# One attention and mixture-of-experts layer: the last weighing ahead of four scatters, the routing tables interleaved with the experts' inner values, two waits of TensorE moved

## The reference

```python
x = x + attention(layernorm(x))
x = x + experts(layernorm(x))
```

```python
sim1 = q @ k_l.T ; sim2 = q_l @ k_l.T ; sim3 = q_l @ k.T
attn1, attn2, attn3 = softmax(sim1), softmax(sim2), softmax(sim3)
out = attn1 @ pinv(attn2) @ (attn3 @ v)     # pinv: 6 Newton-Schulz steps
out = out + conv(out)                        # 13 taps along the tokens, per head
out = out.reshape(b, n, 1024) @ w_fc + b_fc
```

## Time and profile before

| | us |
|---|---|
| median of three runs | 1142.69 |
| lowest and highest | 1137.94, 1143.32 |
| the profiled execution, its own time | 1141.43 |
| its span, first to last instruction | 1139.7 |
| mean granted TensorE clock over the span | 0.992 |
| TensorE busy | 1093.7 |
| VectorE busy | 634.5 |
| ScalarE busy | 303.3 |
| GpSimd busy | 301.2 |

### The profile page before, as it was taken

How to read it: one execution, slowest core, us unless ns; L and a number is a source line. 1 busy time by engine, 2 the same in 40 slices (tenths; PEclk the granted TensorE clock), 3 DMA queues, 4 the chain that set the end, 5 groups by cost and what they waited for, 6 DMA issues and landing times.

```text
span 1139.7 us, 22844 instructions
## 1 busy us (share of the span) xinstructions
PE 1093.7 (96%) x9168; PEld 908.3 (80%) x9168; DVE 634.5 (56%) x1353; ACT 303.3 (27%) x457; POOL 301.2 (26%) x298
## 2 busy tenths in 40 slices
PE   4999999999989999999999999889999999999996
PEld 4887888888888756766776767768888888899996
DVE  7467666555478575686677677662323333244442
ACT  4433223332234422332243233221111111111110
POOL 6000000000200022234643553542232332334343
PEclk9999999999999999999999999899999999999999
DMA  9200000001200040322322134343333333321321
GB/s 340 112 1 1 1 1 1 1 1 38 58 3 0 22 167 28 104 75 61 137 75 85 66 98 131 108 131 76 50 50 51 47 53 48 42 39 36 47 25 12
DMA packets 48540, 68.94 MB, mean 60 GB/s; under 512 B 7872, under 2 KB 41792, under 8 KB 47424
## 3 DMA queue, kind: packets, MB, share of 16 engines
q1 hardware_dynamic: 34720, 47.50, 13.1%
q0 software_dynamic: 13296, 16.92, 8.7%
q10 hardware_dynamic: 432, 3.24, 0.7%
HBM read 42.10 MB, written 26.46 MB: 60 GB/s over the span
## 4 chain that ended last, share of the span: by engine, by line
PE 88%; DVE 6%; issue 2%; POOL 2%; ACT 1%; POOLq 0%; DVEq 0%
PE ps L1770 21%; PE ps L1793 11%; PE ps L1641 10%; PE ps L1694 10%; PE ps L1353 9%; PE ps L1392 9%; PE ps L1686 5%; PE ps L1507 1%; PE ps L1753 1%; PE ps L1327 1%; PE ps L1526 1%; ACT mem L695 1%; PE ps L1407 1%; PE ps L1608 1%; PE ps L1627 1%
## 5 line engine op out<-in xcount | busy, mean ns | idle before, releaser
L1770 PE MATMUL ps<-mem 128*128 128x256 f32 (+1 forms) x1504 | 260.8, 329 | 0.0
L1770 PEld LDWEIGHTS ps<-mem 128*128 128x128 f32 x1504 | 233.4, 192 | 21.2
L569 POOL DMA_INDIRECT out<-mem x71 | 123.9, 1745 | 256.5 <-DVE mem L1229 190.3
L1793 PE MATMUL ps<-mem 128*128 x568 | 136.9, 385 | 5.7 <-DVE mem L1221 3.4
L1221 DVE TENSOR_TENSOR mem<-mem,ps 128x512 f32<-128x512 f32 x71 | 48.8, 687 | 164.7 <-PE ps L1770 144.7
L539 POOL TENSOR_TENSOR mem<-mem,small 128x1024 f32<-128x1024 f32 x36 | 68.6, 1904 | 238.6 <-DVE small L1158 108.7
L1641 PE MATMUL ps<-mem 128*128 128x512 f32 x288 | 129.7, 594 | 1.3 <-DVE mem L1032 1.3
L775 ACT ACTIVATE mem<-ps 128x512 f32<-128x512 f32 x71 | 42.4, 597 | 316.4 <-PE ps L1770 316.4
L1694 PE MATMUL ps<-mem 128*128 128x256 f32 x512 | 120.7, 390 | 0.0
L1793 PEld LDWEIGHTS ps<-mem 128*128 128x128 f32 x568 | 105.4, 193 | 18.7 <-issue 6.3
L1392 PE MATMUL ps<-mem 128*128 128x256 f32 x512 | 117.5, 383 | 0.6 <-ACT mem L649 0.6
(11 more groups left out here) (226 smaller groups left out, 1291.7 us busy)
## 6 DMA issues: line engine op xcount, KB each, us to landing
mem<-w_gu SPq DMA_DIRECT2D x9, 1024.0 KB, 5.9
mem<-xs_d SPq DMA_DIRECT2D x22, 260.0 KB, 2.8
mem<-x SPq DMA_DIRECT2D x8, 512.0 KB, 8.0
mem<-x SPq DMA_DIRECT2D x32, 128.0 KB, 2.3
out<-mem SPq DMA_DIRECT2D x32, 128.0 KB, 1.7
mem<-w_down SPq DMA_DIRECT2D x8, 512.0 KB, 5.8
xnt_d<-mem ACTq DMA_DIRECT2D x3, 1056.0 KB, 5.0
mem<-xnt_d SPq DMA_DIRECT2D x3, 1056.0 KB, 5.0
```

Of the source, the lines that this page charges most:

```text
L569: pool.indirect_dma_start(out=out_rows, out_offset=bass.IndirectOffsetOnAxis(ap=rows[:, D + 1:D + 2].bitcast(U32), axis=0), in_=ys[:, r % ...
L1770: mm = pe.matmul(bank(2 * c + n % 2)[:, i * size:(i + 1) * size], w[:, k, c, f * P:(f + 1) * P], xst[:, a % 2, k, 0:size], start=(k == 0), ...
L1793: mm = pe.matmul(bank(down_bank(a, b))[:, 0:D], hid[:, u, i * size + b * P:i * size + (b + 1) * P], w_d_s[:, e, f], start=(f == 0), stop=( ...
```

## The change

Five places are edited; no instruction is added or taken away on TensorE, VectorE or GpSimd, apart from where waits stand.

1. GpSimd (line 557 on): the scatters of a step that is 35 or 36 go one step later. By `PLACED` these are the eight DMAs of group 5 and no others. So `weigh(35)` and `add_bias(29)` now stand ahead of the first four of them (tiles 0 and 1 of the group), and `add_bias(30)` ahead of the other four. The two loops over groups and halves change places; the order of all other scatters stays as it was.
2. VectorE: `table` is cut in two, `whole_items` (its first six operations) and `table` (the other ten). For the units, `hidden_out(2)` now stands between the two, where it stood behind both.
3. VectorE: `units_taken` and the tiles' table leave their place ahead of `expert_weights(FIRST + 1)` (item 4) and go behind `hidden_out(5)`, in the first unit. The wait for `d_tiles` goes to the first block of item 23.
4. TensorE, landmark stage: in the turn m = 1, `c1_max_columns(3)` goes from between the halves of `c1_ut(1)` to behind the second.
5. TensorE: the wait for `p_pm` goes from ahead of the first `c2_sim` to ahead of the second.

```diff
@@ gpsimd
+            def sent_at(g, h):
+
+                i = PLACED[g] + (h if g < LATE else 0)
+                return i + 1 if QT - 1 <= i <= QT else i
+
             for i in range(STEPS):
                 if 1 <= i <= QT:
                     weigh(i - 1)
                 if y_tile(i) is not None:
                     add_bias(y_tile(i))
-                for h in range(2):
-                    for g in range(NG):
-                        if PLACED[g] + (h if g < LATE else 0) == i and 2 * h < GROUPS[g][1]:
+                for g in range(NG):
+                    for h in range(2):
+                        if sent_at(g, h) == i and 2 * h < GROUPS[g][1]:
                             scatter(g, 2 * h)
                             scatter(g, 2 * h + 1)
@@ vector
-            def table(rows, up, shift, count, eid, row, done):
+            def whole_items(up, shift):
 
                 ch.link(dve.tensor_scalar(te.bitcast(I32), n_e, float(up), None, ALU.add))
...
                 ch.link(dve.tensor_tensor(te, ends, nt, ALU.subtract))
+
+            def table(rows, eid, row, done):
+
                 ch.link(dve.scalar_tensor_tensor(out=tc, in0=te, scalar=-float(rows), in1=base, op0=ALU.mult, op1=ALU.add))
@@ vector
             sizes()
-            table(2 * P, 0, 8, NU, u_eid, u_row, "d_units")
+            whole_items(0, 8)
             hidden_out(2)
+            table(2 * P, u_eid, u_row, "d_units")
             rows_weighed(0)
...
             hidden_out(3)
-            units_taken()
-            table(P, P - 1, 7, NT, t_eid, t_row, "d_tiles")
             expert_weights(FIRST + 1)
             rows_weighed(1)
             hidden_out(4)
-            dve.wait_ge(s("d_tiles"), 1)
             for n in range(BLOCK[FIRST], NSTEP):
                 a, h = STEP_OF[n]
                 if h == 0:
                     rows_weighed(a - 1)
                 hidden_out(n)
+                if n == BLOCK[FIRST]:
+                    units_taken()
+                    whole_items(P - 1, 7)
+                    table(P, t_eid, t_row, "d_tiles")
+                if a + 2 == FIRST + NU and h == 0:
+                    dve.wait_ge(s("d_tiles"), 1)
@@ tensor, landmark stage
                 c1_ut(m, 0)
-                if more:
+                if more and m > 1:
                     c1_max_columns(m + 2)
...
                 c1_ut(m, 1)
+                if m == 1:
+                    c1_max_columns(m + 2)
@@ tensor, ahead of the token stage
-            pe.wait_ge(s("p_pm"), NQ // 4)
             pe.wait_ge(s("c2_g1a"), NQ // 2)
             pe.wait_ge(s("c2_g1b"), NQ // 2)
...
             def token_step(i):
+                if i == 1:
+                    pe.wait_ge(s("p_pm"), NQ // 4)
                 if i < QT:
                     c2_sim(i)
```

## The result

The changed kernel takes 1134.19 us, the median of six runs (1133.93 to 1135.69); the kernel before has 1142.06 beside it. The ratio is 0.9938, with a 95% interval of 0.9922 to 0.9954: 7.1 us, or 0.62%, less (the two medians are 7.9 us apart). On another occasion, beside the last experiments, it was 0.9935 (0.9919 to 0.9952); one of the eleven runs of the kernel before there took 2291.07 us, and the ratio leaves it out. The forecast was 1135.0.

What follows compares the result with a forecast made beforehand. TensorE, running matmuls for 1093.7 of 1139.7 us, was taken as the bound. Terms -1.2 + 0.4 - 2.05 + 0 - 3.75 = -6.6 gave 1134.8 from 1141.43, stated as 1135.0; range 1131.5 to 1140.0.

Steps and rivals of the forecast that it cites:

- Edit 5, forecast -1.2: Start of token stage: `c2_sim(0)` starts right behind the last projection and the first softmax chain moves along; -1.2 us.
- Edit 4, forecast +0.4: Landmark stage, pair 3's transposes: TensorE wins 1.2 us, then idles some 1.5 waiting for `b_sub`; +0.4 us.
- Edit 1, forecast -2.05: Last convolution and group 7's transposes: scores 3.8 us earlier, less one clock fall of 1.75; -2.05 us.
- bound of no wait for a landing: Group 7's normalising: best case without waiting for scattered data to land and without a clock fall; -5.6 us.
- Edit 2, forecast 0: Ahead of `down(2)`: it still waits for the weighing, and the later `d_units` is covered; 0 us.
- Edit 3, forecast -3.75: Ahead of `down(4)`: it starts 2.0 us earlier and a clock fall of 1.75 goes; -3.75 us.
- a fall of the clock: Behind TensorE's idle spans: where the clock falls, a span costs 1.7 to 3.5 us beyond its length.
- the second rival: Around 721 us: the clock falls for as long as before, since light matmuls follow; 1136.5 us, chance 0.15.
- six idle spans of over 0.9 us: TensorE after start-up: 1.90, 1.35, 2.17, 2.3, 2.43 and 1.0 us, the last touched by no edit.

Runs made afterwards that it cites:

- Edit 1's execution: Only GpSimd's scatters of group 5 put one step later, on the kernel before: ratio 0.9979 (0.9962 to 0.9996).
- The two variants: Changed kernel with pair 3's transposes unmoved and `rows_weighed(0)` ahead of the units' `table`: 0.9895 to the kernel before; the same with `hidden_out(2)` back behind the table: 0.9940.
- The run of edit 5: Only the wait for `p_pm` moved to ahead of the second `c2_sim`, on the kernel before: ratio 0.9978 (0.9966 to 0.999).
- the split: Changed kernel with pair 3's transposes unmoved and the two DMAs of group 5's first tile kept ahead of the last weighing: 1131.24 us, 0.9908 to the kernel before.

## Why the prediction was right

Its sum was -6.6 and the profiled executions give -7.1. That they are so close is in part luck: the changed kernel's other profiled execution spans 1131.0 us, -8.7, because the clock did not fall behind `down(2)`'s wait there. What speaks for the prediction is that each step's mechanism was found. Step by step:

- **Edit 5, forecast -1.2, measured -1.33** in the change and alone. `c2_sim(0)` is right behind the projection, and the softmax chain moved along.
- **Edit 4, forecast +0.4, measured +0.3.** The step that decided it was to follow the chain to `b_sub`. The profile before shows 1.90 us of idle time to win; the new one shows it shrunk to 0.5 at 102.7 and grown by 1.5 at 113.7, with line 926 as the releaser. The shape of the argument was right, but it left out one thing. Where edit 4 is absent, the clock fell behind the 1.9 us in three of eleven profiled executions. Edit 1's execution over 99 to 105 us, and then the kernel before's (granted clock 0.72 and 1.00, behind the busy times):

```profile
99.00:105.00 6.00, 4.60 (x15) 3.79 (x16) 4.11 (x8) 0.00 (x0) 0.00 (x0) 0.72 0.00 0
```

```profile
99.00:105.00 6.00, 4.62 (x24) 4.08 (x25) 4.56 (x9) 0.60 (x1) 0.00 (x0) 1.00 0.00 0
```

  That is 6.0 x 0.28 = 1.7 us. In the three with edit 4 it did not fall at either place. Three in eleven of 1.7 us is 0.46, about what the edit costs, so on average it may be worth nothing either way; the runs can't tell (0.9979 to 1.001). Nor do they tell whether it touches the pseudo-inverse stretch, where the three executions with edit 4 took 285.35 to 285.62 us and nine of the eleven without it less.
- **Edit 1, forecast -2.05, measured -2.5.** The mechanism was right in each link: the convolution without a gap, the fourth scatter at 717.49 (forecast 717.65, moved by the 1.0 us of the earlier edits), ScalarE waiting for a DMA, and the single fall. The fourth scatter released its reader 2.5 us after its start, and the scores came 4.2 us earlier instead of 3.8: the fourth scatter was 0.16 earlier, landed 0.1 sooner, and the transposes followed ScalarE by 0.06 and not 0.25. There is luck in the landing: the scatters of the first tile, of which the second started at 714.97, held the first half of the normalising until 718.96, 4.0 us from that start. Had the pair of the second tile taken as long, the transposes would have come some 1.5 us later. The term's bound of no wait for a landing is out (by the prediction's own 1.6 it should have read -5.4 and not -5.6). By the rows' ends (717.49 + 0.96 = 718.45 for the fourth) ScalarE could have begun the second half at 718.5; it began at 720.01, and both halves' idle time is put to the DMA. The Trainium skill, Perfetto Trace Analysis, "DMA Instruction — SWDGE (GPSIMD)", says that such a row ends with the descriptors and not with the data. This trace agrees, with 1.5 us between the row's end and the reader's start.
- **Edit 2, forecast 0, measured 0.03.** The wait is 2.26 instead of 2.29 and has the same releaser. The two variants show why: the weighing has to come ahead of the table as well. SyncE's first load of a unit's rows starts at 753.33, 3.4 earlier than before where `down(2)` is 3.5 earlier, so the later `d_units` costs nothing that matters.
- **Edit 3, forecast -3.75, measured -3.62,** 1.93 of it the wait and 1.69 the clock, in the change; alone it was 3.61. The table fits into VectorE's idle time with 0.81 us to spare, where I had reckoned 0.2 at the least.

What the prediction mis-sized without harm: it priced a fall of the clock at its full loss. The run of edit 5 shows that the long one at 718 us cost only 2.0 of its 3.4, because VectorE was the next to be waited for. And whether a gap of 1.9 to 2.3 us brings a fall differs from execution to execution, where the forecast took it as given. The single fall behind group 7's transposes came in three of the four profiled executions with this order on the chips where ScalarE did not stand still (both of the changed kernel, and edit 1 alone); in the fourth, with the weighing ahead of the table, it was the long one, 6.8 us at half clock. That was the second rival, held at 0.15. The prediction also counted six idle spans of over 0.9 us behind the start-up; it passed over the 1.3 and 1.4 us put to "issue" in the pseudo-inverse, whose stretch differs by 1.65 us from execution to execution.

## What to carry to other kernels

Where an in-order list is the bound, price an idle span by what is late next and not by its length: of five spans that the edits aim at, one paid in full (edit 5), two paid in part (edits 1 and 3), one came back elsewhere (edit 4), and one stayed because its instruction waits for two values and only one was moved (edit 2). Look for such pairs: the weighing's move and edit 2's, each worth next to nothing alone, took away a wait of 2.3 us and the fall of the clock that sometimes follows it. In this kernel taking away 1.9 us of idle time brought 3.6 (edit 3), because the clock had fallen behind it. And before a difference of 1 or 2 us in time is put to a change, look in the trace for the stretch where it arises: of the split's 3.0 us, 1.1 arose in the profiled execution where nothing was changed.

## What the runs showed of the hardware

- The granted clock fell to 1.2 GHz behind the idle span of 1.9 us in the landmark stage in three of eleven executions, behind `down(2)`'s waits of 2.1 to 2.3 us in seven of eleven, and behind `down(4)`'s of 2.4 to 2.7 us in all five. A single fall cost 1.65 to 1.75 us of full-speed work.
- A span's length alone does not tell. Behind the 1.35 us ahead of the first scores (five executions) and the 1.5 us that edit 4 makes (three) the clock never fell; ahead of group 7's scores it fell behind shorter ones, 1.15 and then 0.78 us in the changed kernel and 1.29 in the split one. With the same order of instructions in that stretch one execution had a fall twice as long as the others. Why is not shown.
- An indirect DMA of GpSimd occupies that engine for 0.96 us. In the changed kernel's execution one pair of them released its reader 2.5 us after the start of its second, and the pair before it 4.0 us after.
- On one of the chips ScalarE stood still for 2.3 to 5.2 us at a time, four to six times in each of four profiled executions, in the token stage and at the start of the experts', ended by nothing that the profile can name. The ten executions on other chips show no such wait. The kernel before was 6 us slower there (1148.32 against 1142.06). It was not found out why.
